# Expert exponentials and masks by two heads at a time in a Perceiver layer kernel

## The reference

```
q = (hidden_states @ Wq).reshape(b, t, 2, H, RET // 2)
sim = jnp.einsum('btphn,hkpn->pbthk', q, keys)
sc, ix = jax.lax.top_k(sim, KPH)
...
scores, pk = jax.lax.top_k(all_sc, KPH)
idx = jnp.take_along_axis(all_ix, pk, axis=-1)
de = down_embed[idx]
ue = up_embed[idx]
w = jnp.einsum('btd,bthkd->bthk', hidden_states, de)
w = jax.nn.silu(w) * jax.nn.softmax(scores, axis=-1)
experts_states = jnp.einsum('bthk,bthkd->btd', w, ue)
mlp = jax.nn.silu(hidden_states @ Wg + bg) * (hidden_states @ Wu + bu) @ Wd + bd
return mlp + experts_states
```

## Time and profile before

| | us |
|---|---|
| median of three runs | 868.83 |
| lowest, highest | 868.0, 869.57 |
| profiled execution | 869.66 |
| its span | 867.9 |
| PE busy in the span | 840.7 (97%) |
| DVE, ACT, POOL busy | 576.1, 441.0, 349.9 |

### The profile page before, as it was taken

The page is one execution under the profiler, slowest core; times in us unless marked ns, Lnnn a source line. Parts: engine busy times, 40 slices in busy tenths (PEclk is TensorE's granted clock), DMA queues, the critical chain, the costliest instruction groups (busy, mean ns, idle before and its releaser), DMA issues.

```text
span 867.9 us, 17399 instructions
## 1 busy us (share of the span) xinstructions
PE 840.7 (97%) x6329; PEld 782.9 (90%) x6329; DVE 576.1 (66%) x1536; ACT 441.0 (51%) x1029; POOL 349.9 (40%) x361
## 2 busy tenths in 40 slices
PE   5999999999999999999999999999999999998998
PEld 3999999999999999999999999998977689986886
DVE  7454647566576878656576665777777547766886
ACT  5665454554556464644645545455435434344553
POOL 5742634534463655746454344313301310003443
PEclk9999999999999999999999999999999999999999
DMA  6554427576467757576675664787577676842310
GB/s 215 183 176 164 151 104 238 192 233 226 176 224 256 255 207 280 203 232 201 223 242 205 235 207 163 264 342 256 195 250 298 292 303 273 358 141 102 98 50 25
DMA packets 71126, 183.04 MB, mean 211 GB/s; under 512 B 6353, under 2 KB 19585, under 8 KB 65025
## 3 DMA queue, kind: packets, MB, share of 16 engines
q1 hardware_dynamic: 70944, 181.90, 59.0%
q10 hardware_dynamic: 96, 0.02, 0.0%
HBM read 130.00 MB, written 50.86 MB: 208 GB/s over the span
## 4 chain that ended last, share of the span: by engine, by line
PE 85%; DVE 7%; DMA 4%; issue 2%; ACT 2%; SPq 0%; POOL 0%; DVEq 0%; ACTq 0%
PE pJ L1660 15%; PE pJ L1661 14%; PE pJ L1662 14%; PE pV L1806 7%; PE pS L1784 4%; PE pT L1792 3%; PE pS L1792 3%; PE pS L1660 2%; PE pT L1784 2%; PE pS L1662 2%; PE pS L1661 2%; DMA w_split<-wvst 2%; PE pX L1696 1%; PE pV L1660 1%; PE pV L1661 1%
## 5 line engine op out<-in xcount | busy, mean ns | idle before, releaser
L1660 PE MATMUL pJ<-WV,XT 128*128 128x256 f32 x544 | 158.5, 291 | 0.0
L1661 PE MATMUL pJ<-WV,XT 128*128 128x256 f32 x544 | 153.8, 283 | 0.0
L1662 PE MATMUL pJ<-WV,XT 128*128 128x256 f32 x544 | 153.7, 283 | 0.0
L862 ACT ACTIVATE SP<-SP,xneg 128x768 f32<-128x768 f32 (+1 forms) x96 | 85.8, 895 | 119.3 <-DVE xneg L1235 119.3
L1660 PE MATMUL pJ<-XT,WK 128*128 128x384 f32 (+1 forms) x384 | 126.9, 330 | 3.6 <-DVE XT L1135 1.4
L1662 PE MATMUL pJ<-XT,WK 128*128 128x384 f32 (+1 forms) x384 | 125.2, 326 | 0.0
L1661 PE MATMUL pJ<-XT,WK 128*128 128x384 f32 (+1 forms) x384 | 125.1, 326 | 0.0
L1135 DVE TENSOR_TENSOR KT<-pJ,KT 128x384 fp32r<-128x384 f32 x96 | 51.2, 535 | 89.8 <-ACT KT L839 89.3
L1660 PEld LDWEIGHTS pJ<-WV,XT 128*128 128x128 f32 x544 | 104.1, 191 | 0.2 <-issue 0.2
L1661 PEld LDWEIGHTS pJ<-WV,XT 128*128 128x128 f32 x544 | 104.2, 192 | 0.0
L1662 PEld LDWEIGHTS pJ<-WV,XT 128*128 128x128 f32 x544 | 104.0, 191 | 0.0
(11 more groups left out here) (397 smaller groups left out, 2153.8 us busy)
## 6 DMA issues: line engine op xcount, KB each, us to landing
WS<-w_split SPq DMA_DIRECT2D x14, 2048.0 KB, 8.8
WV<-wv_split SPq DMA_DIRECT2D x20, 1024.0 KB, 7.2
WK<-wk_split SPq DMA_DIRECT2D x40, 512.0 KB, 4.5
w_split<-wkst SPq DMA_DIRECT2D x40, 512.0 KB, 3.6
w_split<-wvst SPq DMA_DIRECT2D x40, 512.0 KB, 3.9
XA<-w_split SPq DMA_DIRECT2D x4, 2048.0 KB, 13.0
xraw<-in_ctx SPq DMA_DIRECT2D x7, 768.0 KB, 6.4
wk_split<-WK SPq DMA_DIRECT2D x8, 512.0 KB, 4.0
```

The source lines that it names most:

```text
L862: ac.activation(SP[:, I % 2, h, 0:w], SP[:, I % 2, h, 0:w], ACT.Exp, bias=xneg[:, I % 2, h:h + 1], scale=XSC, accum_out=total).then_inc(c_ ...
L1660: te.matmul(dst, a(HI), b(HI), start=start, stop=False)
L1661: te.matmul(dst, a(HI), b(LO), start=False, stop=False)
L1662: return te.matmul(dst, a(LO), b(HI), start=False, stop=stop)
```

## The change

The exponential and the mask work on one bank, so on two heads, at a time. Each half of select signals `s_gd` by itself; each half of exponential and mask waits for and signals its own half (`s_gexp` and `s_md` now count two per tile), and each half of the next select waits for its own. GpSimd's head sum waits for both masks.

```diff
@@ gpsimd @@
-                pool.wait_ge(s_md, e + 1)
+                pool.wait_ge(s_md, 2 * e + 2)
@@ scalar, front(e) @@
-                act.wait_ge(s_gd, e + 1)
-                if e >= 1:
-                    act.wait_ge(s_md, e)
-                ac.activation(EW, pJ[:, :, :].rearrange("p a n -> p (a n)"), ACT.Exp).then_inc(s_gexp, 1)
+                for i in range(2):
+                    act.wait_ge(s_gd, 2 * e + 1 + i)
+                    if e >= 1:
+                        act.wait_ge(s_md, 2 * e - 1 + i)
+                    ac.activation(EW[:, 512 * i:512 * i + 512], pJ[:, i, :], ACT.Exp).then_inc(s_gexp, 1)
@@ vector, mask_weights(e) @@
-                dve.wait_ge(s_gexp, e + 1)
-                if e >= 1:
-                    dve.wait_ge(s_hs, e)
-
-                ve.scalar_tensor_tensor(out=MW, in0=pT[:, :, :].rearrange("p a n -> p (a n)"), scalar=8.0, in1=EW,
-                                        op0=ALU.is_gt, op1=ALU.mult).then_inc(s_md, 1)
+                for i in range(2):
+                    dve.wait_ge(s_gexp, 2 * e + 1 + i)
+                    if e >= 1 and i == 0:
+                        dve.wait_ge(s_hs, e)
+                    half_ = slice(512 * i, 512 * i + 512)
+                    ve.scalar_tensor_tensor(out=MW[:, half_], in0=pT[:, i, :], scalar=8.0, in1=EW[:, half_],
+                                            op0=ALU.is_gt, op1=ALU.mult).then_inc(s_md, 1)
@@ tensor, select_(e) @@
-                if e >= 1:
-                    pe.wait_ge(s_gexp, e)
-                    pe.wait_ge(s_md, e)
                 for i in range(2):
+                    if e >= 1:
+                        pe.wait_ge(s_gexp, 2 * e - 1 + i)
+                        pe.wait_ge(s_md, 2 * e - 1 + i)
                     te.matmul(pJ[:, i, :], SEL[:, e, :], GX[:, HI, 2 * i:2 * i + 2, :, :], start=True, stop=False)
                     te.matmul(pJ[:, i, :], SEL[:, e, :], GX[:, LO, 2 * i:2 * i + 2, :, :], start=False, stop=True)
-                    last = te.matmul(pT[:, i, :], SEL[:, e, :], RT[:, 2 * i:2 * i + 2, :, :], start=True, stop=True)
-                last.then_inc(s_gd, 1)
+                    te.matmul(pT[:, i, :], SEL[:, e, :], RT[:, 2 * i:2 * i + 2, :, :], start=True, stop=True).then_inc(s_gd, 1)
```

## The result

| | before | after |
|---|---|---|
| median, 12 runs each | 868.91 us | 866.72 us |
| ratio after to before | | 0.9974, 95% interval 0.9962 to 0.9987 |
| the same pair in a later series on another occasion | | 0.9993, 0.9979 to 1.0007 |
| span of the first profile | 867.9 us | 863.5 us |

The changed kernel is faster, by 1.1 to 3.3 us in the first series; the second doesn't tell it from no change. The profiles show one reason why two series can differ: the part of the program ahead of the expert loop is the same instruction for instruction, and it scatters by more than the change is worth. Select(0) starts at 783.30 and 783.36 us in two profiles of the kernel before, at 780.41 and 782.85 in two of the changed one. From select(0) on, both kernels repeat to 0.05 us.

The account below looks back on a forecast made before the run. Early expert-loop turns were taken as bound by the select, Exp, mask round trip, late turns by TensorE. Gains of 1.34 + 0 + 0.37 us, say 1.70, off the median 868.83 gave 867.1 us, range 866.2 to 868.8.

Parts of the forecast that it names:

- What binds: Expert loop: early turns wait on the select, Exp, mask round trip; a late turn has TensorE busy all its 4.70 us.
- The price of a half: Mask on VectorE: two halves step 1.20 us against 1.13 whole, so each mask costs 0.07 us more.
- The upper bound: Most a mask in halves could cost extra on VectorE: 1.17 us, from the 512-column split of the up rows, 1.23 long.
- the slower rival: VectorE's queue in turns 5 to 12 becomes the bound: 2.4 us slower, 871.2 us; chance 0.07.
- Term 1: First turns: VectorE reaches L1633(0) 1.55 us earlier; less 0.21 for three masks, TensorE gains 1.34 us at turn(5).
- The gain that isn't kept: Early turns: select(2) starts 2.15 us earlier, but VectorE's unbroken chain to L1638 stops TensorE keeping all of it.
- Term 2: Late turns: VectorE's loop becomes 4.67 us against TensorE's 4.65, losing 0.16 us over eight turns, all hidden: 0 us.
- Term 3: End of the loop: L1633(14) starts 0.37 us earlier, then held by Tanh(14), and all 0.37 reaches the end.
- Dearer halves: Mask halves on VectorE don't overlap, 0.25 us more per mask: gain only 0.8 us, time 868.0; chance 0.20.
- vanishing waits: TensorE's 3.1 us of select waits simply vanish, plus 0.37 at the end: gain 3.5 us, 865.4; chance 0.05.
- signals that do nothing: Select's first half is not seen earlier, only the masks' extra cost remains: 0.35 us slower, 869.2; chance 0.04.
- within 0.2%: Whole kernel: measured time within 0.2%, or 1.74 us, of no change; given a chance of 0.55.

Follow-up runs that it names:

- select_waits_whole: Changed kernel, but the next select waits at its start for both halves of exponential and mask; loop 79.87 us, as in the changed kernel's second profile.
- mask_quarters: Changed kernel, but each half mask is done as two operations of 256 columns; loop 80.49 us, 0.9984 of the kernel before.
- no_last_sum: Changed kernel without GpSimd's second addition for the last tile, whose weights are then wrong; loop 79.67 us, 0.9974 of the kernel before.

## Why the prediction was right

Forecast: 867.1 us, 1.70 less. Measured: 866.72, which is 2.19 less than the median before, and 1.50 less where the change acts. That the medians lie so near the forecast is in part luck, as they moved by more than the loop did; the forecast stands by its terms. By its steps:

- **What binds.** Right: early turns by a round trip, late turns by TensorE. Behind turn(5) TensorE is busy 55.83 of 56.70 us.
- **The price of a half.** x = 0.07 taken, 1.19 - 1.13 = 0.06 measured; duration 0.68 and step 0.60 as the turned_lo row said. The upper bound was badly understood: of the 1.23 us, 0.55 was not what 512 columns cost but a wait for GpSimd, which no mask had. Its place beside GpSimd's L777 in the timeline would have told. With that known the slower rival had lost one of its two grounds.
- **Term 1.** L1633(0) ahead by 1.55, measured 7.87 - 6.39 = 1.48. Mask(1) behind GpSimd's sum, select(2) waiting, L1638 still setting turn(5): all as written. Less three masks, 1.34 forecast and 1.28 measured.
- **The gain that isn't kept.** Select(2) came 2.08 us earlier against select(0) (forecast 2.15) and 1.28 were left at turn(5). select_waits_whole shows it from the other side: select(2) may come later at no cost.
- **Term 2.** 0, and mask_quarters shows that even three times the extra cost (0.19 and not 0.06) is hidden there but for 0.09 us at most.
- **Term 3.** This is the term that was mis-sized: 0.37 forecast, 0.22 measured. L1635(14) was 0.38 earlier, held by Tanh as forecast. The step that failed is "So the 0.37 reaches the end": GpSimd's last addition, also earlier, now met a VectorE operation with two SBUF inputs and held it 0.17 us. Without that addition 0.38 arrives (no_last_sum).
- **Rivals.** Dearer halves, VectorE as the bound, vanishing waits (3.5 us) and signals that do nothing were all refuted by the same rows.
- **The range of outcomes.** The forecast lay 0.04 us inside "within 0.2%". The first series says 0.26%, the second 0.07%, the loop 0.17%. Between the series lie the scatter ahead of the loop, up to 3.7 us between profiles, and the granted clock, which was reduced in none of the changed kernel's first twelve runs and in four of its second. The prediction had neither in its sum.

## What to carry to other kernels

When an operation is halved so that its reader can start, follow the reader's reader: here the next matmuls started 2 us earlier and 1.28 us were left, and the half signals to them could be dropped at no cost, because the chain on VectorE sets the pace. Ask of the engine that paces a stretch which work in its queue could stand elsewhere; moving two pieces gave more than the halves did. And before a long duration is taken as a price, look what GpSimd does at that moment.

## What the runs showed of the hardware

A VectorE operation on two SBUF inputs that starts while a GpSimd addition is under way ends a fixed time behind it. With 256 columns it ended 0.27 to 0.29 us later, so 0.42 became 0.59 to 1.02, depending on how much of the addition was left; with 512 columns 0.54 later, so 0.68 became 1.23. A 32-column operation with one SBUF input, 0.17 us long, became 0.72 and ended 0.03 later. In both kernels GpSimd's addition took 0.73 to 0.75 where it started first, as at 854.86, and 0.84 to 0.86 where the low part of `WC` on VectorE was already running, as in the rows of the kernel before. Operations with one input in PSUM (the masks, turned_lo) kept their 0.68 to 0.69 beside it. The Trainium skill says of this, in Perfetto Trace Analysis, section Optimizing Scalar/DVE Operations, that GpSimd and VectorE share an SBUF read port; the rows agree. The same section's 125 ns of overhead per VectorE instruction on PSUM isn't what a half cost: 0.06 us here.
